# Rows of beta and gamma computed in four column groups of TensorE, with VectorE adding the partial rows of the fusion

## The reference

```python
x = x + _L0_xcond_ref(_layernorm(x), ctx_1024, cond_1024, ..., fusion_W, fusion_b, ln_gamma, ln_beta)
x = x + _L0_ffn_ref(_layernorm(x), W_fc, ln_w, ln_b, W_proj)
```

```python
z = sigmoid(x @ W.T + b); h_tilde = tanh(x @ W.T + b)
h = linear_scan(clip(1 - z), z * h_tilde)      # along the tokens
h = h + previous h (from layer 1 on); h = (h - mean) * rsqrt(var + 1e-5) * gamma + beta
out = concat(h_fwd, h_bwd) @ fusion_W.T + fusion_b
```

## Time and profile before

| | |
|---|---|
| three runs, median | 1549.22 us |
| the profiled execution, its own time | 1553.49 us |
| its span in the trace | 1551.2 us |
| granted TensorE clock, mean | 0.999 |
| busy of the span | PE 99%, PEld 81%, DVE 86%, ACT 66%, POOL 65% |

### The profile page before, as it was taken

How to read it: one execution, slowest core, us unless ns; L and a number is a source line. 1 busy time by engine, 2 the same in 40 slices (tenths; PEclk the granted TensorE clock), 3 DMA queues, 4 the chain that set the end, 5 groups by cost and what they waited for, 6 DMA issues and landing times.

```text
span 1551.2 us, 22809 instructions
## 1 busy us (share of the span) xinstructions
PE 1529.5 (99%) x7690; PEld 1257.9 (81%) x7690; DVE 1328.7 (86%) x1885; ACT 1023.0 (66%) x1689; POOL 1008.0 (65%) x1136
## 2 busy tenths in 40 slices
PE   7999999999999999999999999999999999999999
PEld 4877888888888888888888878888888888888887
DVE  7888899999899989999888888787878888787876
ACT  6888879898687898687987543544444444444454
POOL 4765666667868677776778745465565556565566
PEclk9999999999999999999999999999999999999999
DMA  5111231413302011213133551030202020111101
GB/s 177 35 55 55 76 102 35 163 41 109 122 29 95 29 62 62 95 55 109 48 116 135 193 189 41 1 109 1 89 21 89 21 85 25 62 48 36 34 14 41
DMA packets 72865, 112.65 MB, mean 73 GB/s; under 512 B 5160, under 2 KB 37928, under 8 KB 69679
## 3 DMA queue, kind: packets, MB, share of 16 engines
q1 hardware_dynamic: 72750, 111.21, 21.3%
HBM read 73.43 MB, written 37.76 MB: 72 GB/s over the span
## 4 chain that ended last, share of the span: by engine, by line
PE 52%; DVE 1%; ACT 0%; issue 0%; POOL 0%; DVEq 0%; POOLq 0%
PE ps L592 15%; PE ps L611 15%; PE ps L561 11%; PE ps L496 6%; PE ps L516 1%; PE ps L530 1%; PE ps L574 1%; PE ps L621 1%; PE ps L634 0%; DVE bnp L1106 0%; PE ps L645 0%; DVE H L1094 0%; DVE H L1095 0%; DVE yb L1086 0%; ACT ntok L812 0%
## 5 line engine op out<-in xcount | busy, mean ns | idle before, releaser
L496 PE MATMUL ps<-AH,WH 128*128 128x512 f32 x896 | 367.4, 410 | 6.7 <-DVE H L1095 6.0
L496 PE MATMUL ps<-AL,WH 128*128 128x512 f32 x896 | 351.4, 392 | 0.0
L496 PE MATMUL ps<-AH,WL 128*128 128x512 f32 x896 | 349.7, 390 | 0.0
L1646 POOL TENSOR_TENSOR acq<-acq,sq 128x512 f32<-128x512 f32 x120 | 183.6, 1530 | 156.2 <-ACT sq L932 155.7
L1086 DVE TENSOR_TENSOR_SCAN yb<-ab,ps 128x512 f32<-128x512 f32 x192 | 232.6, 1211 | 23.8 <-POOL ab L1522 17.3
L1531 POOL TENSOR_TENSOR H<-H,yb 128x512 f32<-128x512 f32 x192 | 245.5, 1290 | 9.4 <-DVE yb L1086 1.1
L919 ACT ACTIVATE g<-ps 128x512 f32<-128x512 f32 x128 | 76.5, 597 | 251.3 <-PE ps L592 251.3
L800 ACT ACTIVATE yb<-ps,ncnd 128x512 f32<-128x512 f32 x224 | 158.5, 707 | 103.1 <-PE ps L496 99.2
L1283 DVE SCALAR_TENSOR_TENSOR gl<-g,wcol,gh 128x512 fp32r<-128x512 f32 x118 | 123.5, 1047 | 97.1 <-ACT gh L929 96.1
L496 PEld LDWEIGHTS ps<-AH,WH 128*128 128x128 f32 x896 | 168.7, 188 | 43.3 <-DVE H L1095 8.6
L496 PEld LDWEIGHTS ps<-AL,WH 128*128 128x128 f32 x896 | 168.3, 188 | 37.2
(11 more groups left out here) (174 smaller groups left out, 3330.5 us busy)
## 6 DMA issues: line engine op xcount, KB each, us to landing
hs_scratch<-H SPq DMA_DIRECT2D x16, 1024.0 KB, 5.5
hc<-hs_scratch SPq DMA_DIRECT2D x32, 512.0 KB, 4.4
xr<-in_x SPq DMA_DIRECT2D x32, 256.0 KB, 4.5
out<-ob SPq DMA_DIRECT2D x32, 256.0 KB, 2.2
xbuf<-in_x SPq DMA_DIRECT2D x7, 1024.0 KB, 8.1
RAW<-in_wt SPq DMA_DIRECT2D x16, 256.0 KB, 6.5
stg<-in_fct SPq DMA_DIRECT2D x16, 256.0 KB, 3.4
stg<-in_pjt SPq DMA_DIRECT2D x16, 256.0 KB, 2.8
```

Of the source, the lines that this page charges most:

```text
L496: r = e.matmul(GATE[i % 3][:], w[:, q, m * 128:(m + 1) * 128], a[:, q, :], start=(n == 0), stop=(n == 11))
L1646: e.tensor_tensor(acq[b % 2][:], acq[b % 2][:], sq[:], ALU.add).then_inc(f_s2, 1)
```

## The change

The matrices `bet32` and `gb` become 32 columns wide for each quarter of the contraction, with zeros behind the first one or two columns. The four matmuls of V1, V2, G0 and G1 no longer accumulate: each writes its own 32 partitions of the PSUM bank (`32 * q`), so each has its own group of 32 columns of the array. For V1 and V2, ACT copies all 128 partitions of the bank, and `shift` contracts over all 128 (four partial rows and zeros), which sums them. For G0 and G1, VectorE copies the first partial rows to SBUF, adds the other three one by one, each add waiting for the one before, and then adds the sum to the fusion bias; ACT's `take_rows` is gone, and the bank is free after VectorE's fourth instruction (`s_gs`). The orders of the engines are otherwise kept.

```diff
+    bet32 = sb(p1, "bet32", [128, KC, 32])
+    gb = sb(p1, "gb", [128, KC, 32])
@@ TensorE: claim, shift, fold_row, add_rows
             elif u[0] == "G":
-                e.wait_ge(s_gr, u[1] + 1)
+                e.wait_ge(s_gs, 4 * u[1] + 4)
...
-            p = slice(0, 1) if l in BY_ROW else slice(0, 128)
...
-                r = e.matmul(RING[n % 5][:, m:m + 1], bw[l][p, m * 128:(m + 1) * 128], ones[p, :], start=True, stop=True)
+                r = e.matmul(RING[n % 5][:, m:m + 1], bw[l][:, m * 128:(m + 1) * 128], ones[:], start=True, stop=True)
...
-            e.wait_ge(d_c, 48)
+            e.wait_ge(s_b32, 2)
             for q in range(KC):
                 e.wait_ge(d_w[l][q], 16)
-                r = e.matmul(RING[n % 5][0:1, :], bet[:, q:q + 1], RAW[l][:, q, :], start=(q == 0), stop=(q == KC - 1))
+                r = e.matmul(RING[n % 5][32 * q:32 * q + 32, :], bet32[:, q, :], RAW[l][:, q, :], start=True, stop=True)
...
-            e.wait_ge(s_gb, 2)
+            e.wait_ge(s_gb, 3)
             for q in range(KC):
-                r = e.matmul(RING[n % 5][0:2, :], gb[:, q, :], xbuf1[:, q, :], start=(q == 0), stop=(q == KC - 1))
+                r = e.matmul(RING[n % 5][32 * q:32 * q + 32, :], gb[:, q, :], xbuf1[:, q, :], start=True, stop=True)
@@ ScalarE: take_row; take_rows and its two calls (slots 6 and 8) removed
-            e.activation(bw[l][0:1, :], RING[BANK[("V", l)] % 5][0:1, :], ACT.Copy).then_inc(s_rc, 1)
+            e.activation(bw[l], RING[BANK[("V", l)] % 5][:], ACT.Copy).then_inc(s_rc, 1)
@@ VectorE: bias_rows
+            dst = (raw0[0:2, :], xbuf1[0:2, 0, :])[h]
+            part = RING[BANK[("G", h)] % 5]
             e.wait_ge(s_gp, h + 1)
+            if h == 0:
+                e.wait_ge(s_bp, L - 1)
+            e.tensor_copy(dst, part[0:2, :]).then_inc(s_gs, 1)
+            for q in range(1, KC):
+                e.wait_ge(s_gs, 4 * h + q)
+                e.tensor_tensor(dst, part[32 * q:32 * q + 2, :], dst, ALU.add).then_inc(s_gs, 1)
+            e.wait_ge(s_gs, 4 * h + 4)
...
-            e.tensor_tensor(fbb[0:2, :], RING[BANK[("G", h)] % 5][0:2, :], fbb[0:2, :], ALU.add).then_inc(s_gv, 1)
+            e.tensor_tensor(fbb[0:2, :], dst, fbb[0:2, :], ALU.add).then_inc(s_gv, 1)
@@ GpSimd: minus, columns_of_rows, start
             e.wait_ge(d_c, 48)
+            e.wait_ge(s_b32, 1)
+            e.tensor_copy(bet32[:, :, 0], bet[:]).then_inc(s_b32, 1)
...
             e.wait_ge(d_c, 48)
+            e.wait_ge(s_gb, 1)
...
         e.memset(ones[:], 1.0).then_inc(s_c, 1)
+        e.memset(gb[:], 0.0).then_inc(s_gb, 1)
+        e.memset(bet32[:], 0.0).then_inc(s_b32, 1)
@@ SyncE: put_rows
-            e.wait_ge(s_gr, 2)
+            e.wait_ge(s_gs, 8)
```

More of the change, by code:

```diff
@@ L254, in pixart_block @@
     fbb = sb(ctx, "fbb", [128, 512])
-    gb = sb(ctx, "gb", [128, KC, 2])
     rl = sb(ctx, "rl", [128, NB, 2, 4])
@@ L365, in pixart_block @@
         sem(n) for n in ("s_wh", "s_y", "s_t", "s_nt", "s_xn", "s_ah", "s_h", "s_abs"))
-    s_ph, s_sg, s_gr, s_rc = sem("s_ph"), sem("s_sg"), sem("s_gr"), sem("s_rc")
+    s_ph, s_sg, s_rc = sem("s_ph"), sem("s_sg"), sem("s_rc")
     f_xh, f_g, f_hi, f_sq, f_ev = (sem(n) for n in ("f_xh", "f_g", "f_hi", "f_sq", "f_ev"))
@@ L372, in pixart_block @@
         sem(n) for n in ("s_al", "s_xs", "s_xa", "s_xm", "s_ss", "s_th"))
-    s_fo, s_gv, s_ct = sem("s_fo"), sem("s_gv"), sem("s_ct")
+    s_fo, s_gv, s_gs, s_ct = sem("s_fo"), sem("s_gv"), sem("s_gs"), sem("s_ct")
     f_sh, f_sp, f_x1, f_b1, f_a1, f_n1, f_xl = (
@@ L380, in pixart_block @@
         sem(n) for n in ("s_c", "s_wp", "s_p", "s_v", "s_rs", "s_nb", "s_xr", "s_xb", "s_pp", "s_pl"))
-    s_w0 = sem("s_w0")
+    s_w0, s_b32 = sem("s_w0"), sem("s_b32")
     s_gb, s_ws = sem("s_gb"), sem("s_ws")
@@ L1026, in _ @@
             gates(job(s - 2), 3)
-            if s == 6:
-                take_rows(0)
             norm(tail_b(s - 3), 0)
@@ L1038, in _ @@
             feature("h", tail_b(s - 4), 3)
-            if s == 8:
-                take_rows(1)
             feature("h", tail(s - 3), 0)
```

## The result

The changed kernel is slower: 1555.31 us (median of 7 runs, 1553.36 to 1555.90) against 1549.54 us for the kernel before, run beside it. The ratio is 1.0035, with a 95% interval of 1.0025 to 1.0044, that is +3.9 to +6.8 us. The forecast was 1551.0 us, no change that can be told; the time lies 0.1 us inside the upper end of the range, 1547.6 to 1555.4. By the prediction's own measure (3.1 us) the change can be told: it is the outcome "slower", to which it gave 0.27. The profiled executions are only 2.0 us apart (1553.49 and 1555.47 us). The profile before was 2.55 us above the slowest of the seven runs of its kernel; why is a part of what follows.

The account below looks back on a forecast made before the run. TensorE (busy 99%) was taken as the bound, with new waits paid in full. Terms -1.2 (V1), -0.2 (V2), +2.55 (G0) and +0.65 (G1) sum to +1.8 us: 1551.0 us on the median, range 1547.6 to 1555.4.

Parts of the forecast that it names:

- outcome "slower": Whole kernel: measured slower than before by more than the 3.1 us that can be told; chance 0.27.
- D: Extra VectorE time in each `bias_rows`, five instructions instead of one: 3.0 us, bounds 2.3 and 3.45.
- S: TensorE time saved per four-matmul fold by overlapping column groups: 1.28 us at the high clock, at most 2.57.
- five places: Each four-matmul fold: eight passes started in order pair up as 1, (1,2), (2,3), (3,4), 4, saving 1.28 us.
- second rival: All folds: column groups overlap fully, saving 2.57 us each; sum +0.7 us, 1549.9 us; chance 0.25.
- first rival: All folds: column groups don't overlap, saving nothing; sum +4.5 us, 1553.7 us; chance 0.25 for no overlap or worse.
- +0.65: G1: 1.93 us of lateness from VectorE's longer queue, less 1.28 us saved on TensorE; net loss in us.
- D - 0.45 = 2.55 us of new stall: G0: VectorE's added 3.0 us, less 0.45 us slack, delays the second half of `tokens(4, 1)`, costing 2.55 us.
- -1.2: V1: shorter fold lets `mm(0, 0)` start near 16.8 instead of 18.05, gaining 1.2 us; bounds -2.0 and +0.4.
- other bound: V1, +0.4 us: TensorE idle until 15.5 may run twelve matmuls 0.2 us slower each, losing 2.4 us.
- V2: Layer 2 fold: gains only 0.2 us, because `tokens(0, 1)` waits for VectorE's forward scan; 0.23 us at most.
- I put the same difference on the median: Sum: differences from the profiled execution (1553.49 us) applied unchanged to the median of 1549.22 us, 4.3 us lower.

Follow-up runs that it names:

- V1 alone: Column groups for V1 only, with V2, G0 and G1 as in the kernel before: ratio 1.0006 (0.9997 to 1.0015) to the kernel before.
- G0 and G1 alone: Changed kernel with V1, V2, `shift` and `take_row` as before; G0 and G1 in column groups with VectorE's five instructions: ratio 1.0021 to before, 1553.35 us.
- V1 and V2 alone: Changed kernel with G0, G1, VectorE's one add and ScalarE's copies as before; V1 and V2 in column groups: ratio 1.0005 (0.9996 to 1.0014) to before.
- VectorE's part alone: Kernel before plus a copy and three dependent adds, results unused, ahead of the one add in both `bias_rows`: ratio 1.0042 (1.0029 to 1.0054) to before.
- V1 and V2 alone with the wait behind V1 filled: V1 and V2 in column groups, G0 and G1 as before, plus 6 extra matmuls between V1 and `mm(0, 0)`: ratio 1.0005 (0.9996 to 1.0014) to before.
- changed with the stall at G0 filled: Changed kernel plus 15 extra matmuls between `mm(3, 3)` and `tokens(4, 1)`, where TensorE waits: ratio 1.0018 (1.0009 to 1.0027) to before, 1553.46 us.

## Why the prediction was right in part, step by step

- **What bounds the kernel, and D.** Right. VectorE's five instructions cost 2.98 us against 3.0, and the new wait stood where it was forecast, at `tokens(4, 1)`. With the clock held, C grew by 2.7 us against the 2.55 of the prediction.
- **S, the saving on TensorE.** Mis-sized: 1.28 us by five places, measured 3.52 - 0.99 = 2.53 us at G1. All eight passes fit in two places, the upper bound and the second rival; the first rival, no overlap, is refuted. V1 and V2 could not use it; at G0 1.06 us of it was waited away for POOL and the rest for VectorE; at G1 it turned +0.65 into -0.7. With S right, the sum 1.93 - 2.53 = -0.6 meets it.
- **The clock behind the stall.** Missing, a term put at nothing without a reason. The step "D - 0.45 = 2.55 us of new stall" stopped at the wait; TensorE came out of it at its low level and paid 1.5 us more. The prediction had rows with both speeds, those of V1, and used them for V1 alone.
- **V1.** The step "-1.2" took the profile's V1 for typical. The gain is there against that execution and not in the run times (V1 alone: 1.0006, from 0.9997 to 1.0015): in other executions V1 runs at the high clock, and then VectorE's low weights set the pace in either form. Where V1 in groups ended in a wait and `mm(0, 0)` ran at the low clock, as in the changed kernel, it took from that call to `shift(1)` 20.10 - 15.40 = 4.70 us instead of 21.02 - 18.05 = 2.97; this is the loss that the prediction named as its other bound.
- **V2.** Right as a bound: 0.2 us (6.38 to 6.21 us). What was left out is the price of an idle TensorE, the fall of the clock that some executions show there.
- **The base of the sum.** "I put the same difference on the median" failed. On the profile, +1.8 was close to +2.0 by luck: the missed clock (+1.5) and the term of G1, 1.35 us too high by the small S, nearly cancel. Seven runs lay at 1548.7 to 1550.9 with the profile at 1553.5, and none of the 87 later runs of before went over 1552.53; the early stretch of such a profile was no base for a term at the start. On a typical execution the terms are 0 for V1, -0.2 for V2, +4.2 at G0 and -0.7 at G1, +3.3 us; the last two, +3.5, agree with G0 and G1 alone (+3.3, from 2.0 to 4.6). The rest up to +5.8, the difference of the medians, these terms do not hold. V1 and V2 alone cost +0.8 (-0.6 to +2.2), so the two parts sum to +4.1, which is inside the interval of the whole change (+3.9 to +6.8) but below its middle. The mean granted clocks fit the same split: 0.9973 over the changed kernel's runs, 0.9987 with G0 and G1 alone and 0.9985 with V1 and V2 alone, against 0.9998 in before beside these two. Which falls of the clock make the last 1 to 2 us stays open.
- **The range.** It held the time by luck. Its upper end, 1555.4, was put there for most of the first rival, column groups that don't overlap. They overlap fully; what brought the time there is the fall of the clock, which is in no term of the prediction, and the early part, where the -1.2 us of V1 did not come.

## What to carry to other kernels

Before work is moved from the bound engine to one that is less busy, read the queue of the other at that place and find the next thing in it that the bound engine waits for: 3 us put ahead of such an instruction made the stretch at G0 4 us longer, the same 3 us behind it left it 0.3 us shorter than before. Add to a new wait of TensorE the price of the low clock behind it. And compare a profile with the runs: if it lies outside them, find out which stretch is odd before a term is taken from it.

## What the runs showed of the hardware

- Four fp32 matmuls of 32 columns each, in four column groups, take 0.99 us to the next stream, where four that accumulate take 3.52 us: 3.6 times. The full-width stream behind them starts right then (126.55 to 127.54), so no cost of leaving the groups is to be seen.
- TensorE was at its low level behind waits of 3.68 and 3.70 us (changed; G0 and G1 alone) and of 2.21 us (VectorE's part alone) at G0, and behind a wait of 2.13 us behind V2 in two profiles (V1 and V2 alone with the wait behind V1 filled; changed with the stall at G0 filled). Behind V2 it stayed high after 1.70 to 1.75 us, in four profiles. It was also low near 54 us, in a stretch of short transposes with no wait over 0.61 us, in three of fourteen profiles.
- A fall cost 1.5 us at G0, 1.3 us near 54 us and 1.4 us behind V2 (from `mm(1, 0)` to `tokens(0, 1)` 4.84 us against 3.43 us). Fifteen extra matmuls in the wait prevented it at G0.
- The granted clock of the windows read 1.00 at the start while passes took twice their time; there the distance between weight loads tells the level better.
